# Loading the convolution weights from ScalarE's queue instead of SyncE's

## The reference

```python
def _L0_tok_ref(x, gamma, beta, W, b):
    lu, ru, ld, rd = _shifts(x)
    concat = jnp.concatenate((x, lu, ru, ld, rd), axis=1)
    mean = jnp.mean(concat, axis=(1, 2, 3), keepdims=True)
    var = jnp.var(concat, axis=(1, 2, 3), keepdims=True)
    normed = (concat - mean) * jax.lax.rsqrt(var + EPS)
    normed = normed * gamma[None] + beta[None]
    y = jax.lax.conv_general_dilated(normed, W, window_strides=(PATCH, PATCH), padding='VALID', ...)
    ...
def step(S, qkv):
    qt, kt, vt = qkv
    S = S + LR * jnp.einsum('bd,be->de', vt, kt)
    out = jnp.einsum('de,be->bd', S, qt)
    return (S, out)
...
h = _L0_tok_ref(x, L0_tok_gamma, L0_tok_beta, L0_tok_W, L0_tok_b)
h = jnp.concatenate([jnp.broadcast_to(cls_tok, (h.shape[0], 1, h.shape[2])), h], axis=1)
h = h + _L0_attn_ref(_layernorm(h, axis=-1), L0_attn_Wq, L0_attn_Wk, L0_attn_Wv, L0_attn_memory0)
h = h + _L0_ffn_ref(_layernorm(h, axis=-1), L0_ffn_W, L0_ffn_b)
```

## Time and profile before

| | |
|---|---|
| median of 3 runs | 222.69 us (222.07, 222.69, 222.77) |
| profiled execution | 222.06 us |
| its span | 219.8 us |
| PE busy | 198.4 us, 90% of the span |
| DVE, ACT, POOL busy | 153.1, 129.2, 152.6 us |
| moved by DMA | 25.90 MB |

### The profile page before, as it was taken

How to read it: one execution, slowest core, us unless ns; L and a number is a source line. 1 busy time by engine, 2 the same in 40 slices (tenths; PEclk the granted TensorE clock), 3 DMA queues, 4 the chain that set the end, 5 groups by cost and what they waited for, 6 DMA issues and landing times.

```text
span 219.8 us, 5078 instructions
## 1 busy us (share of the span) xinstructions
PE 198.4 (90%) x1566; PEld 168.4 (77%) x1566; DVE 153.1 (70%) x762; ACT 129.2 (59%) x315; POOL 152.6 (69%) x126
## 2 busy tenths in 40 slices
PE   0699998999899999999999999999999999998710
PEld 0489897877688889888888888899888888887600
DVE  3649884462487685768696587786687678699791
ACT  4322547798433545556755574655665585577983
POOL 1029948796982799969899939948999452363651
PEclk9999999999999999999999999999999999999975
DMA  5999991934113005234135242022012112200346
GB/s 140 395 417 425 418 422 73 252 128 123 51 24 140 4 3 161 54 100 141 23 84 172 79 134 49 3 49 51 7 41 51 25 27 48 49 4 13 70 113 149
DMA packets 17074, 25.90 MB, mean 118 GB/s; under 512 B 1576, under 2 KB 13551, under 8 KB 16920
## 3 DMA queue, kind: packets, MB, share of 16 engines
q1 hardware_dynamic: 16300, 25.06, 35.6%
q10 hardware_dynamic: 748, 0.51, 0.9%
HBM read 19.65 MB, written 5.92 MB: 116 GB/s over the span
## 4 chain that ended last, share of the span: by engine, by line
PE 69%; DMA 9%; DVE 8%; ACT 5%; SPq 3%; issue 3%; POOL 1%; POOLq 0%; ACTq 0%; DVEq 0%
PE conv L553 32%; PE vr_ps L597 12%; PE outs L624 9%; DMA images<-x_rows 9%; PE first_ps L607 9%; PE turn L587 4%; DVE dve L1215 2%; PE conv L561 2%; ACT scaled L761 1%; ACT values L791 1%; SPq L472 1%; DVE state L966 1%; DVE state L958 1%; DVE ln_stats L995 1%; DVE g_t L941 1%
## 5 line engine op out<-in xcount | busy, mean ns | idle before, releaser
L553 PE MATMUL conv<-scaled,wt 128*128 128x256 f32 (+3 forms) x432 | 111.6, 375 | 7.3 <-DMA wt<-weight 6.9
L455 POOL TENSOR_TENSOR scaled<-rows,gam 128x832 f32<-128x832 f32 (+1 forms) x54 | 84.0, 1577 | 18.0 <-DMA rows<-x_windows 17.8
L553 PEld LDWEIGHTS conv<-scaled,wt 128*128 128x128 f32 x432 | 72.0, 193 | 15.4 <-DMA wt<-weight 6.9
L791 ACT ACTIVATE values<-vr_ps,rstd 128x256 f32<-128x256 f32 x76 | 36.1, 475 | 61.2 <-PE vr_ps L597 52.1
L1290 POOL TENSOR_TENSOR rstd<-var,powers 128x8 f32<-128x8 f32 (+2 forms) x20 | 30.4, 1521 | 27.2 <-DVE var L978 27.1
L958 DVE TENSOR_TENSOR state<-first_ps,state 128x128 f32<-128x128 f32 x76 | 22.1, 291 | 29.4 <-PE first_ps L607 24.5
L799 ACT ACTIVATE images<-images,ln_shift,ln_gain 128x128 f32<-128x128 f32 x83 | 38.4, 488 | 0.9 <-DVE ln_shift L1035 0.8
L1280 POOL TENSOR_TENSOR g_low<-g_t,g_high 128x512 fp32r<-128x512 f32 x21 | 26.8, 1276 | 7.5 <-ACT g_high L778 7.5
L597 PE MATMUL vr_ps<-w_high,g_low 128*128 128x256 f32 x77 | 30.9, 402 | 0.5 <-ACT values L791 0.5
L947 DVE BATCH_NORM_STATS2 ln_stats<-images 128x6 f32<-128x128 f32 x85 | 23.5, 284 | 6.0 <-ACT images L785 5.9
L966 DVE TENSOR_TENSOR state<-second_ps,state 128x128 f32<-128x128 f32 x76 | 21.5, 283 | 2.1
(11 more groups left out here) (190 smaller groups left out, 275.3 us busy)
## 6 DMA issues: line engine op xcount, KB each, us to landing
rows<-x_windows SPq DMA_DIRECT2D x12, 864.0 KB, 4.8
out<-images SPq DMA_DIRECT2D x40, 128.0 KB, 2.4
images<-x_rows SPq DMA_DIRECT2D x4, 832.0 KB, 14.5
images<-x_rows SPq DMA_DIRECT2D x1, 1040.0 KB, 14.0
images<-x_rows SPq DMA_DIRECT2D x1, 624.0 KB, 20.6
rows<-x_windows SPq DMA_DIRECT2D x1, 448.0 KB, 6.2
gam<-gamma SPq DMA_DIRECT2D x1, 422.5 KB, 6.8
bet<-beta SPq DMA_DIRECT2D x1, 422.5 KB, 7.3
```

Source lines behind the costliest of these rows:

```text
L455: return eng.tensor_tensor(scaled[:, s, at + skip:at + N], window[:, skip:N], gains.unsqueeze(2).to_broadcast([P, N - skip, B]), ALU.mult)
L553: last = pe.matmul(conv_ps[g % 2][:, at:at + n * B], held, scaled[:, s, a % RING:a % RING + n], start=first, stop=(g < EARLY and s >= TOP ...
L791: act.activation(values[:, t % VALUE_SLOTS].rearrange("p a e -> p (a e)"), vr_bank(t)[:, 0:2 * E], ACT.Identity, scale=rho_of(t)).then_inc ...
```

## The change

The DMA that loads `wt` (128 partitions x 640 float32, 320 KB) leaves SP's stream, where it stood third, and becomes the first DMA in ACT's stream. Its source, its destination and its semaphore are the same, and PE's wait for it too. Nothing else is edited; the line numbers between the two places go down by one.

```diff
             sp.dma_start(gam_first[:], first_gamma).then_inc(first_gamma_in, 16)
             sp.dma_start(rows[:, 0, 0:N], x_windows[:, 0, 0:N]).then_inc(row_in[0], 16)
-            sp.dma_start(wt[:], weight).then_inc(weight_in, 16)
             sp.dma_start(rows[:, 0, N:2 * N + 1], x_windows[:, 0, N:2 * N + 1]).then_inc(first_right_in, 16)
...
+            act.dma_start(wt[:], weight).then_inc(weight_in, 16)
             act.dma_start(cls_col[:], cls_tok.rearrange("(e o) -> e o", o=1)).then_inc(cls_in, 16)
             act.dma_start(cls_h[B:P], cls_tok.partition_broadcast(B)).then_inc(cls_in, 16)
```

## The result

The changed kernel took 224.28 us (median of 4 runs, 224.10 to 224.72) against 222.72 us for the kernel before, a ratio of 1.0078 with a 95% interval of 1.0044 to 1.0111. Forecast was 222.4, with a range from 221.6 to 223.2, within 0.3% of the kernel before. The profiled execution took 224.10 us, its span grew from 219.8 to 221.9 us.

The account below looks back on a forecast made before the run. The prediction took PE to bound the steady part and DMA of the images, then DVE's statistics, the first 34.38 us. Terms 0 + 0 - 0.3 + 0 = -0.3 us turned the median 222.69 into 222.4, range 221.6 to 223.2.

Parts of the forecast that it names:

- What bounds the kernel: First 40 us: chain runs through the images' DMA and DVE's statistics, reaching PE at 34.38; the weights are not in it.
- One sign at the start: DMA windows, 1.75 to 2.25 us: a share near 1 and more than 82 GB/s were expected after the change.
- SP's and ACT's issues: DMA issue slots: SP's later issues come 0.47 us earlier, covered, worth 0; ACT's added issue fits its waits, cost 0.
- The weights travel in the unfilled time: DMA before 5 us: weights use unfilled engine time, so later landings come 0.3 us earlier; term -0.3 us.
- PE may be up to 0.3 late and has 0.72. Cost 0: PE at the second scaled plane: lateness up to 0.3 us is covered by its 0.72 us wait for the sums.
- The paragraph on the clock: PE's rise from 1.2 to 2.4 GHz near 13 us: if 0.7 us later, PE loses another 0.35, still under 0.72.
- PE's start: PE's first multiply, 6.91 before: expected at 7.0 to 7.6, ended by the scaled plane instead of wt; cost 0.
- rival 3: First multiply (L553) too late because weights are served ahead of row 0: slower, 223.7 at a start of 8.5; chance 0.10.
- price rule: Rival 3, first multiply at s: (s + 1.8 - 9.37) plus half of (s - 6.91), less 0.72 free.
- Rival 2: Early DMA: no gain, or alternating queues cost up to 0.4 us; 222.7 to 223.1; chance 0.22.
- Rival 1: Early DMA: the gain is whole, weights cost the engines nothing; 0.78 us faster, 221.9; chance 0.20.
- The sign list: Marks expected in the profile after, among them PE's wait for the sums at 34.1 and DVE's 28.16 start at 27.9.

Follow-up runs that it names:

- m_after: Changed kernel with PE's fifth plane of group 3 done ahead of the wait for the sums; 221.95 us, ratio 0.9972 to the kernel before.
- m_again: m_after run once more, in the second group beside m_before; 221.95 us, ratio 0.9978 to the kernel before.
- m_before: Kernel before, wt still third in SP's queue, with the same reordering of PE's work as m_after; 221.57 us, ratio 0.9961.
- cls_late: m_after with only the cls_col and cls_h loads held back until the right half of row 0 has landed; 221.26 us, ratio 0.9941.
- e1_fill: Changed kernel with six unused multiplies of ones put ahead of PE's wait for the sums; 222.64 us, ratio 0.9997 to the kernel before.
- e2_delay3: Kernel before with three more statistics instructions on DVE ahead of the sums; 225.33 us, ratio 1.0100.
- e3_sp_first: Kernel before with the wt load kept in SP's queue but first instead of third; 222.61 us, ratio 1.0003.
- e4_act_third: Changed kernel with the wt load third in ACT's queue, behind cls_col and cls_h; 222.22 us, ratio 0.9958 to the kernel before.
- e5_small_late: Changed kernel with ACT's four small loads issued only after row 0's right half landed, terms cleared before them; 225.4 us, ratio 1.0116.
- cls_late_before: m_before with cls_col and cls_h held back as in cls_late, wt third in SP's queue; 221.71 us, ratio 0.9965.

## Why the prediction was wrong

**What bounds the kernel:** right. The chain is the one that was read, the weights are not on it, and the loss arises on it. One sign at the start failed: in 1.75 to 2.25 the engines moved 77 GB/s, not more than 82.

**SP's and ACT's issues:** right. SP's right half of row 0 was issued at 1.64, ACT's wt at 0.73, own at 2.25. ACT stood 0.64 us for cls_h ahead of L886, and had 4.1 us in hand behind it.

**"The weights travel in the unfilled time", -0.3 us:** the first half was right, the conclusion wrong. The stretch to 5 us filled up from 181 to 277 GB/s, more than assumed. But the step "the bytes ahead of the images do not change, so what matters is how much unfilled time they take up" took for granted that the stretch behind stays full. It went from a share of 1.01 to 0.67. The term measured about 0: 217 against 218 GB/s until 8.25 us, and the start of DVE's statistics that should have come at 27.9 came at 28.65. The trace of m_after, with the same loads, has that start at 27.88, but the time of its program is no lower than with the weights in SP's queue (m_again and m_before), so no run shows the gain of 0.3. I had considered what cls_h and cls_col wait for behind the weights, and not what waits for them; cls_late showed that SP's supply suffers from them.

**"PE may be up to 0.3 late and has 0.72. Cost 0":** this is the step that failed. I asked what happens if PE comes late. It came 0.85 us early at the sums (32.81 instead of 33.66). I took the wait of 0.72 us for free slack that could only shrink or stay, and did not ask what a longer one costs. The paragraph on the clock treated only its first rise. Grown to 2.03 us (0.85 by the earlier PE, 0.46 by the later sums), the wait brought the clock down, which cost 1.68 us on the chain: a term that the sum had at 0. e1_fill and e2_delay3 show it from both sides: the loss goes when the wait is filled, and comes in the kernel before when the wait is made longer. It is not certain in each execution: in 5 of 16 the changed kernel kept its clock and lost nothing. How often it falls could not be read from the trace of the kernel before; that a longer wait might have a price was never asked. The seven high executions of the kernel before have the lower mean clock too, though the wait is 0.72 and 1.03 us in its two traces; none of the seven has a trace, so where their clock was low is open.

**PE's start:** forecast 7.0 to 7.6, measured 6.80; DVE's first plane 5.63, only 0.4 later than before. The weights did not push the start of DVE back to 6.9, the worst case. PE was then not idle before the second plane, which DVE began 0.76 us earlier (7.53 instead of 8.29), and row 1 reached POOL at 14.45 instead of 14.96.

**The rivals:** rival 3 has the right sign and the wrong mechanism; a late start is harmless, as e3_sp_first (8.53) and e4_act_third (8.91) show, and its price rule would give them 1.05 and 1.6 us. Half of that price was a rise of the clock that moves back with PE's start; in both it did not (twelve records in 4.28 and 4.26 us instead of 5.42), and PE was at group 1 at 19.36 and 19.72. Rival 2 is nearest for the DMA (nothing gained): its sign, a start of 28.16 that stays or grows, came true with 28.65, but its price of 0 to 0.4 us holds no clock. Rival 1 did not occur. None named a slower time through an earlier engine. **The sign list** at the end had "PE's wait for the sums still there, at 34.1"; the wait was there, at 34.84, and the sign should have had its length.

## To carry to other kernels

Idle time of TensorE ahead of a wait is not free to grow: before making it reach a wait earlier, look how long it will stand there, and put real work that is ready in front of the wait. A median can hide two heaps; where a loss is there in some executions and absent in the rest, compare the mean granted clock of each, and then look for the stretch in windows of a microsecond. A load that is moved to another queue should be judged with the small loads that now stand behind it.

## What was not expected of the hardware

- The clock can fall when PE is already back at work (wait until 34.84, clock 1.00 in 34.5 to 35 and 0.50 in 36 to 39), so it is the work behind a gap that pays. In e5_small_late it fell while PE still stood. In the traces, waits of 2.03, 2.77 and 3.8 us brought it down, waits of 1.64 and 2.16 us did not. With waits of 0.2 to 1.1 us at the sums in their traces, e1_fill, m_after, m_again and m_before have no low mean clock in 44 executions; the kernel before, with 0.72 and 1.03, has 7 in 86.
- Two loads of 32.5 KB together, 128 pieces of 4 bytes and 64 of 512, behind 320 KB in the same queue, took the DMA engines from a share of 1.03 (cls_late) to about 0.7 (five traces) for almost 2 us, although SP had issued loads of over 1 MB (1229 KB in gam, bet and small alone, by 4.5 us). The Trainium skill's "DMA: Bandwidth & Descriptors", section "Issuing engines are not separate DMA queues", says that starting transfers from several engines saves only the time of issuing them. For the moved load alone the bytes until 8.25 us agree (217 and 218 GB/s). With the two small loads held back they do not: the same load in ACT's queue gives 284 GB/s (cls_late) and in SP's queue 243 (cls_late_before), from one trace each, and the times differ by 0.45 us.
- One and the same program brings its sums 0.2 to 0.3 us earlier or later from one execution to the next (34.84 and 35.03; 34.38 and 34.67), and m_after and m_again, the same program on two chips, lie 0.9 us apart (34.13 and 35.02). Differences of that size between two single traces say little.
